# Head 0 of the expert attention: two column groups of the softmax weights turned on TensorE where there were four, the rest by the transposing DMA

## The reference, cut to what matters

```python
    q5 = (x @ Wq).reshape(b, t, H, E, DH)                 # H=8, E=5, DH=64
    q = jnp.einsum('bthed,bthe->bhtd', q5, sd_g)          # gates keep 3 experts of 5
    k = jnp.einsum('bthed,bthe->bhtd', k5, ss_g)
    v = jnp.einsum('bthed,bthe->bhtd', v5, ss_g)
    attn = jax.nn.softmax(jnp.einsum('bhid,bhjd->bhij', q * scale, k), axis=-1)
    out = jnp.einsum('bhij,bhjd->bihd', attn, v)
    o5 = jnp.einsum('bthd,dm->bthm', out, Wo).reshape(b, t, H, E, DIM)
    return jnp.einsum('bthem,bthe->btm', o5, md)
```

## Time and profile before

| | us |
|---|---|
| median of 3 runs | 2636.36 (2632.11 to 2636.94) |
| the profiled execution, its own time | 2637.34 |
| its span | 2635.5 |
| stage `g0_`, its steps | about 1390 to 1930 |
| stage `g1_`, its steps | about 2095 to 2635 |

### The profile page before, as it was taken

One profiled execution on the slowest core, in us unless ns is written; L12 is line 12 of the kernel. 1 busy time (PEld: TensorE's weight loads), 2 busy tenths in 40 slices (PEclk: granted clock), 3 DMA queues, 4 the chain that ended last, 5 costly groups with the idle time before them and its releaser, 6 DMA issues. The chain is left out here.

```text
span 2635.5 us, 55999 instructions
## 1 busy us (share of the span) xinstructions
PE 2365.9 (90%) x21310; PEld 1544.0 (59%) x21310; DVE 2011.4 (76%) x3656; ACT 1500.2 (57%) x2085; POOL 1740.0 (66%) x1704
## 2 busy tenths in 40 slices
PE   6788777888799999999978999999879799999987
PEld 3555534644466667666655666666634556666655
DVE  7998555644677777777669999999567899999974
ACT  4222122332688888888834666666744256666665
POOL 0888300000699999999946888888720378888885
PEclk9898779889799999999989999999979899999998
DMA  1000000000698989889942555555610145555555
GB/s 46 1 1 0 1 24 14 1 24 14 137 160 151 165 145 162 160 151 163 147 112 51 101 100 102 102 97 101 112 43 0 69 78 101 101 102 101 101 103 101
DMA packets 763819, 226.74 MB, mean 86 GB/s; under 512 B 745992, under 2 KB 754696, under 8 KB 763552
## 3 DMA queue, kind: packets, MB, share of 16 engines
q1 hardware_dynamic: 763552, 223.16, 46.2%
HBM read 20.70 MB, written 1.05 MB: 8 GB/s over the span
## 5 line engine op out<-in xcount | busy, mean ns | idle before, releaser
L2302 PE MATMUL banks<-g_w,normed_t 128*128 128x320 f32 x1536 | 495.3, 448 | 17.2 <-DVE g_scratch L2620 10.8
L1557 ACT ACTIVATE g_p<-banks,g_negmax 128x1024 f32<-128x1024 f32 x256 | 285.9, 1117 | 322.4 <-DVE g_negmax L1593 322.4
L1580 POOL TENSOR_TENSOR g_p_lo<-g_p,g_p_hi 128x512 bf16<-128x512 f32 (+1 forms) x256 | 416.0, 1646 | 40.0 <-POOL g_z L2506 19.8
L1785 DVE TENSOR_REDUCE at_negmax<-banks 128x1 f32<-128x1024 f32 x256 | 301.6, 1220 | 153.9 <-PE banks L1697 153.9
L2302 PEld LDWEIGHTS banks<-g_w,normed_t 128*128 128x128 f32 x1536 | 271.6, 190 | 202.6 <-DVE g_scratch L2620 105.4
L1762 POOL TENSOR_TENSOR at_p_lo<-at_p,at_p_hi 128x640 bf16<-128x640 f32 x256 | 356.5, 1411 | 13.1 <-ACT at_p_hi L1750 11.6
L1593 DVE TENSOR_REDUCE g_negmax<-banks 128x1 f32<-128x1024 f32 x256 | 309.9, 1218 | 33.2 <-PE banks L1504 33.2
L1743 ACT ACTIVATE at_p<-banks,at_negmax 128x1024 f32<-128x1024 f32 x256 | 285.4, 1115 | 6.2 <-DVE at_negmax L1785 6.2
L1697 PE MATMUL banks<-at_k_t,at_q 64*128 64x512 f32 x1024 | 258.0, 623 | 17.1 <-POOL at_k_t L2046 8.8
L1504 PE MATMUL banks<-g_k_t,g_q 64*128 64x512 f32 x1024 | 254.4, 615 | 8.2 <-ACT g_p L1557 6.6
L1564 ACT CAST g_p_hi<-g_p 128x512 bf16<-128x512 f32 (+1 forms) x256 | 215.3, 841 | 1.2 <-DMA g_t_lo<-g_p_lo 0.6
(11 more groups left out here) (419 smaller groups left out, 6177.6 us busy)
## 6 DMA issues: line engine op xcount, KB each, us to landing
at_swapped<-at_crossed SPq DMA_DIRECT2D x128, 128.0 KB, 2.8
g_w<-in_ex_w SPq DMA_DIRECT2D x2, 2880.0 KB, 11.5
f_w<-in_W SPq DMA_DIRECT2D x2, 1024.0 KB, 5.7
at_rope<-in_rope SPq DMA_DIRECT2D x1, 2048.0 KB, 10.7
at_t_hi<-at_p_hi SPq DMA_TRANSPOSE x128, 3.7
at_t_lo<-at_p_lo SPq DMA_TRANSPOSE x128, 3.6
g_t_hi<-g_p_hi SPq DMA_TRANSPOSE x128, 3.7
g_t_lo<-g_p_lo SPq DMA_TRANSPOSE x128, 3.7
```

The costliest lines, as they stand in the source:

```text
L1557: self.nc.scalar.activation(self.p[:, j % 2, h, :], self.core.banks[:, 2 * h:2 * h + 2, :], ACT.Exp, bias=self.negmax[:, h:h + 1]).then_in ...
L1580: self.nc.gpsimd.tensor_tensor(self.part(self.p_lo, j, h), self.p[:, j % 2, h, 0:self.WIDTH[h]], self.part(self.p_hi, j, h), ALU.subtract) ...
L1785: self.nc.vector.tensor_reduce(self.negmax[:, j % 2, h:h + 1], self.core.banks[:, first:first + 2, :], AX.XY, ALU.max, negate=True).then_i ...
L2302: nc.tensor.matmul(out[:, 0:ED], core.xt[:, at:at + P], w[:, kind * H + tile // (T * BATCH) * 2 + h, :], start=True, stop=True).then_inc(p ...
```

## The change

The class constant `KEPT` goes from 4 to 2, and what was derived from the half of a row by `CHUNK` (512) is derived from `KEPT`. The comparison at the values' loop picks the kept blocks by their place behind the turned ones. Nothing else is edited; the low halves of the values are made by the same engines as before.

```diff
-    KEPT = CHUNK // P
+    KEPT = 2
     TURNED = 2 * T - KEPT
-    WIDTH = (CHUNK, SEQ)
-    START = (0, CHUNK)
+    WIDTH = (SEQ - KEPT * P, SEQ)
+    START = (0, SEQ - KEPT * P)
@@ __init__
-        self.home = core.ps[self.HOME]
+        self.home = core.ps[self.HOME][:, 0:self.KEPT * P]
-        self.r_hi, self.r_lo = (sb(n, [P, 2, CHUNK], BF16) for n in ("r_hi", "r_lo"))
+        self.r_hi, self.r_lo = (sb(n, [P, 2, self.KEPT * P], BF16) for n in ("r_hi", "r_lo"))
@@ transpose
-            at = CHUNK + k * P
+            at = self.WIDTH[0] + k * P
@@ values
-            if h == 0 and k >= self.KEPT:
-                block = slice((k - self.KEPT) * P, (k - self.KEPT + 1) * P)
+            n = k - self.WIDTH[0] // P
+            if h == 0 and n >= 0:
+                block = slice(n * P, (n + 1) * P)
```

## The result

| us | before | after |
|---|---|---|
| median of the runs | 2636.65 (2632.11 to 2637.58, 4 runs) | 2682.58 (2676.31 to 2687.38, 4 runs) |
| ratio, 95% interval | | 1.0173 [1.0160, 1.0186] |
| the profiled execution, span | 2635.5 | 2685.6 |
| the 26 loops of four steps, sum | 822.0 | 869.7 |

The changed kernel is 46 us slower. The forecast was 2653 us, with a range up to 2674: the sign was right, the size was not. The profiled execution of after, at 2687.38 us, is the slowest of its four.

What follows compares the result with a forecast made beforehand. Each four-step loop was bound first by GpSimd and the DMA (12 us), then by TensorE and VectorE. Loops at + 0.65 us plus stage ends gave + 16.2 on 2636.4: 2653 us, own range 2643 to 2665, 8-in-10 range 2639 to 2674.

Steps and rivals of the forecast that it cites:

- Sizes of the operations: Per step: GpSimd's `pool_lo` of head 0 + 0.49 us, the lo DMA + 0.3, ScalarE's rounding of head 0 + 0.21.
- The loop of + 0.65 us: Four-step loop where TensorE awaits the lo DMA: + 0.49 GpSimd, + 0.3 DMA, - 0.14 plain steps; 20 such loops, + 13.0 us.
- VectorE's floor: In plain steps VectorE takes over as the bound at about 7.46 us, 0.07 below TensorE's 7.53.
- a sign of error: Forecast wrong if plain steps fall below 7.4 us, turning-step waits don't grow, or GpSimd's pause closes.
- the visible wait near 1.4 us: TensorE's wait for the lo DMA in turning steps grows from 0.36 us by 0.8 and 0.22, in all of them.
- the sum: Whole kernel: 13.0 + 1.6 + 1.4 + 1.2 - 1.0 = + 16.2 us over loops, stage ends and unit 0.
- The clock rival: TensorE's granted clock falls behind the longer turning-step wait, 1.7 us each; 2667 us for a third of 24 loops; 12 in 100.
- TensorE's gain shows: `pool_lo` and DMA lateness is absorbed; plain, turning and last-unit steps gain 18 us in all, 2618 us; 7 in 100.
- GpSimd as the bound: GpSimd becomes the bound if `pool_lo` needs more than 0.76 us extra; about + 25 us; 1 in 100.

Runs made afterwards that it cites:

- the relief alone: Kernel before with two transposes and half the subtraction left out, copies of 256 columns, `pool_lo` and DMAs as before: 2630.34 us, ratio 0.9983.

## Why the prediction was wrong

- **Sizes of the operations: right.** `pool_lo` + 0.49 us (forecast 0.49), the lo DMA + 0.4 (0.3), ScalarE's rounding + 0.21.
- **The loop of + 0.65 us: right for its own kind, and not by luck.** Loops without a fall are mostly 32.0 to 32.7 us, and the two regular ones shown have pauses of 1.08 and 1.07 (1.1). Up to the landing a loop costs + 0.80 us (forecast 0.79), behind it - 0.17 (- 0.14). With six idle products per turning step, which take away most of the falls, the kernel is 29 us slower than before, 12 above the forecast.
- **VectorE's floor: wrong.** Plain steps are 7.28 to 7.41 us, not 7.46, below the 7.4 that I had named as a sign of error. I had measured a floor in a trace where TensorE held VectorE back in each step. Shorter plain steps should make the kernel faster, but the relief alone is worth only 5 us; so this miss doesn't explain the 46.
- **The failed step: the visible wait near 1.4 us, and with it the clock, which the sum put at nothing.** I took 0.36 + 0.8 for the later data and 0.22 for TensorE's earlier arrival. In the steady loops the wait is 2.07 to 2.15 us. The later data were sized right: with TensorE's full load put back they make a wait of 1.15 us, 0.8 more than before. The relief was mis-sized: alone, with the data as early as before, it makes the wait 1.16 to 1.2 us, 0.8 more and not 0.22. The last transposes ahead of the wait, before and after (the `v_lo` of these loops start at 1707.64 and 1725.82 us):

```profile
1718.77 0.60 PE L1515 MATMUL banks<-identity,g_p 128*128 128x128 f32 x4
1719.73 0.20 PE L1544 MATMUL banks<-g_v_hi,g_t_hi 128*128 128x65 bf16 x1 [0.36 <-DMA g_t_lo<-g_p_lo]
```

```profile
1736.22 0.38 PE L1515 MATMUL banks<-identity,g_p 128*128 128x128 f32 x2
```

  They end 11.73 us behind `v_lo` before and 10.78 after, 0.95 earlier. Only 0.21 of it are the two transposes of the turning step. The plain step from one step's scores to the next gives 0.25 (7.53 to 7.28), and 0.48 is there already when `v_lo` starts: the scores next to it start 0.50 us behind it before and 0.02 after. The sum didn't carry the relief into the wait; with waits of 2.1 us the clock fell in 14 of 26 loops for 2, and a fall costs 1.6 us.
- **The clock rival: its mechanism happened, its chance was too low.** I gave it 12 in 100, from a wait of 1.4 us and from the earlier trace rows, where one of two waits of 1.61 us was followed by the lower level. The trace before held more on it that I didn't use: in the last loop of each stage TensorE waits for the lo DMA for 2.46 us (at 1846.05) and 2.44 us (at 2549.23), and in the 3.4 us behind them the granted clock is 0.52 and 0.51. 14 of 26 loops had a fall. Its price, 1.7 us per loop, is borne out by 33.8 us for 32.2. With a wait of 2.1 us in the forecast, it would have been the likeliest case.
- **Other rivals.** That TensorE's gain shows is refuted: the relief alone is worth 0.17%. The Trainium skill (Perfetto Trace Analysis, section on the most-contended engine) would start with the engine of the highest occupancy; TensorE is busy 59.31 us of 60, and giving it work back made the changed kernel 16 us faster. The same section judges TensorE's headroom by its weight loads (or by the arithmetic done, as a share of the peak) and not by its busy matmuls; those take 38.71 us of 60 in the earlier trace rows, less than VectorE's 55.95, and this the prediction left out. GpSimd as the bound was refused for the right reason in this kernel, but with the waits gone it comes close to being it (62.2 us per unit).

## What to carry to other kernels

Work taken off the busiest engine doesn't vanish where that engine waits for a chain across others: it turns into a longer wait, so carry every relief into the length of the next wait and then ask what that length does to the granted clock. Where TensorE waits for a DMA each loop, put work that needs no late data into the wait, even a few idle products (17 us here), or take the pause that makes the data late off the path: moving one GpSimd instruction by a step gained 9 us on the kernel before and 43 on the changed one. Measure an engine's floor where nothing holds it back.

## What the runs showed of the hardware

- Over the fourteen profiles, among the waits of TensorE for the lo DMA in the two stages (0.25 us and more, up to 1850 and 2555 us): none of 172 below 1.6 us was followed by the lower clock level within 2 us, 2 of 40 between 1.6 and 1.9 us, 37 of 52 above. Behind these times, where TensorE also waits for other things, 5 of 62 below 1.6 us were, the shortest at 0.9 us. These are counts of this kernel, in which TensorE is otherwise busy; a wait's length alone doesn't settle it: in the changed kernel 2.10 us stands without a fall at 1605.41 and with one at 2462.9 us. What decides between them stays open.
- A fall can lock in. From 1671.8 us the low stretches start at 1671.8, 1705.9, 1740.0, 1774.2, 1808.3 and 1842.4, each 3.4 us long and 34.1 to 34.2 apart, while the loops are 33.8 to 34.8 us long. The Trainium skill (TensorE: Matmul & The Clock Gate, section on HAM oscillation) describes a kernel where a DMA wait in each tile throws the clock back each time; in these six loops the trace agrees, with 33.8 us for 32.2 where no DMA is late besides.
- The transposing DMA lands in 4.1 us at the median, but 23 of the 128 `g_t_lo` took over 4.6 us, up to 6.0; before it was 8 of 128. One of these in front of a turning step made the loop up to 1.4 us longer (33.65 us for 32.2, without a fall). What delays them stays open.
